# Value products in pairs, row maxima by DMA and a reordered start in an attention block (one core)

## The reference

```
q = rmsnorm(x @ q_a_w.T) @ q_b_w.T          # 16 heads of 128 + 64 (rope)
kv_a = x @ kv_a_w.T                          # 64 latent + 16 x 64 rope keys
k_nope, v = split(rmsnorm(kv_a[:64]) @ kv_b_w.T)
main = softmax(q k^T / sqrt(192)) v          # 16 heads, rope on the 64-wide parts
pattern = softmax(pq pk^T / 4) pv            # 16 heads of 16, from sp_q, sp_k, sp_v
y = gate0 * (main @ o_w.T) + gate1 * (pattern @ sp_o_w.T)
x = x + layernorm(y)
out = x + layernorm(FFN(layernorm(x)))       # 256 -> 1024 -> 256, gelu, weights quantised to MXFP4
```

## Time and profile before

| | us |
|---|---|
| median of 3 runs | 852.96 (850.64 to 856.71) |
| the profiled execution | 857.39 |
| its span | 855.6 |
| TensorE busy | 793.0 (93%) |
| VectorE busy | 587.0 (69%) |
| ScalarE busy | 403.5 (47%) |
| GpSimd busy | 429.9 (50%) |

### The profile page before, as it was taken

The page is one execution under the profiler, slowest core; times in us unless marked ns, Lnnn a source line. Parts: engine busy times, 40 slices in busy tenths (PEclk is TensorE's granted clock), DMA queues, the critical chain, the costliest instruction groups (busy, mean ns, idle before and its releaser), DMA issues. The chain is left out here.

```text
span 855.6 us, 12767 instructions
## 1 busy us (share of the span) xinstructions
PE 793.0 (93%) x4928; PEld 456.4 (53%) x4928; DVE 587.0 (69%) x669; ACT 403.5 (47%) x510; POOL 429.9 (50%) x259
## 2 busy tenths in 40 slices
PE   4878899999999999999999999999999999979984
PEld 4654555545545554555555545555555555437863
DVE  3754765666577667757775767577866689994856
ACT  3432344445555555554555455545554455531351
POOL 1414208652865475548555844584486445640233
PEclk9978899999999999999999999999999999999988
DMA  8578363005300530072017201610432413313001
GB/s 214 214 196 277 93 135 71 13 13 130 58 25 14 113 76 12 14 161 63 1 40 160 62 2 54 133 50 12 72 74 79 126 51 98 95 45 81 1 2 49
DMA packets 89024, 68.00 MB, mean 79 GB/s; under 512 B 58178, under 2 KB 67972, under 8 KB 88708
## 3 DMA queue, kind: packets, MB, share of 16 engines
q1 hardware_dynamic: 88964, 67.19, 31.0%
HBM read 41.23 MB, written 17.04 MB: 68 GB/s over the span
## 5 line engine op out<-in xcount | busy, mean ns | idle before, releaser
L991 POOL TENSOR_TENSOR acc<-acc,em 128x1024 f32<-128x1024 f32 x96 | 235.6, 2454 | 96.4 <-ACT em L1049 96.4
L1142 DVE TENSOR_REDUCE m2p<-xb 128x2 f32<-128x1024 f32 x128 | 155.2, 1220 | 79.2 <-PE xb L1300 78.9
L1150 DVE TENSOR_REDUCE m<-xb 128x2 f32<-128x1024 f32 x128 | 155.6, 1219 | 62.5 <-PE xb L1300 62.4
L1040 ACT ACTIVATE ep<-xb 128x1024 f32<-128x1024 f32 x128 | 131.1, 1024 | 112.7 <-PE xb L1300 112.7
L1049 ACT ACTIVATE em<-xb 128x1024 f32<-128x1024 f32 x128 | 131.1, 1024 | 100.7 <-PE xb L1300 91.2
L1335 PE MATMUL pvm<-em,cpair 128*64 128x512 f32 x512 | 138.2, 618 | 0.0
L954 POOL TENSOR_TENSOR rot<-rot,sin 128x512 f32<-128x512 f32 x32 | 40.9, 1279 | 116.7 <-DMA rot<-raw 116.7
L1300 PEld LDWEIGHTS xb<-pq,pk 49*128 49x128 f32 x256 | 23.8, 183 | 100.2 <-issue 81.2
L1346 PE MATMUL pvp<-ep,vp 128*32 128x512 f32 x512 | 68.2, 605 | 0.0
L991 POOL TENSOR_TENSOR acc<-em 128x1024 f32<-128x1024 f32 x16 | 38.9, 2431 | 55.5 <-PE xb L1443 50.9
L1300 PE MATMUL xb<-pq,pk 49*128 49x512 f32 x256 | 64.0, 497 | 0.0
(11 more groups left out here) (279 smaller groups left out, 1284.3 us busy)
## 6 DMA issues: line engine op xcount, KB each, us to landing
rot<-raw SPq DMA_DIRECT2D x128, 64.0 KB, 2.1
pk<-spqk_d SPq DMA_DIRECT2D x48, 128.0 KB, 4.3
sums<-rec_d SPq DMA_DIRECT2D x32, 128.0 KB, 2.9
ctx_d<-ctxr SPq DMA_DIRECT2D x14, 256.0 KB, 2.0
pq<-spqk_d SPq DMA_DIRECT2D x48, 64.0 KB, 2.3
wraw<-wst_d SPq DMA_DIRECT2D x7, 384.0 KB, 6.0
em<-in_o_w SPq DMA_DIRECT2D x1, 2048.0 KB, 7.6
vp<-vp_d SPq DMA_DIRECT2D x8, 256.0 KB, 4.5
```

What stands on the lines that cost most here:

```text
L991: pool.tensor_tensor(acc[:, :, :], before, em[:, j:j + 2, :], ALU.add).then_inc(added, 1)
L1040: act.activation(ep[:, j:j + 2, :], src[:, :, :], ACT.Exp, scale=PAT_SCALE).then_inc(ep_ready, 1)
L1142: dve.tensor_reduce(m2p[:, t, 2 * tp:2 * tp + 2, kt], src[:, :, :], AX, ALU.max).then_inc(x_dve, 1)
L1150: dve.tensor_reduce(m2[:, q, t, :, kt], src[:, :, :], AX, ALU.max).then_inc(x_dve, 1)
```

## The change

1. Row maxima no longer go through TensorE and ScalarE. The tiles mT and pT are gone. Query tiles in pm and mm take every fourth query (`t::4`), so that partition p of `ms` and `msp` holds the maxima of queries 4p to 4p + 3, and a DMA per head (`main_rows`, `pattern_rows`) writes 128 pieces of 16 bytes to one row of `mr` or `pq`. M(0) and M(8) wait for these DMAs (`mr_in`).
2. V of two half steps and PV come together at the end of even half steps.
3. The tiles of a half step are in another order: at odd ones T, pm, M, the further pm, P; at even ones pm, M, two mm, P, T. pm stand mostly at odd ones; two mm come at each even one, with `MM_LATE` 8 in place of 9.
4. The quantising is spread otherwise (`QPLAN`): 39 steps in slots 1 to 7 in place of 31, 32 in slot 8 in place of 39. Its transfers are moved to other places of SyncE's list.
5. The prologue's jobs are in another order (x is transposed first), and `xh`, `xl` are made in two halves; the gates' softmax comes earlier. In slot 0 `sk` and `sv` are made in halves, and in another order.

```diff
@@ prologue: jobs
-    jobs = [("w1T", k) for k in range(NK)] + [("spT", 0), ("spT", 1)]
-    jobs += [("kpT", k, 0) for k in range(NK)] + [("xT", k, 0) for k in range(NK)]
-    jobs += [("kpT", k, 1) for k in range(NK)] + [("xT", k, 1) for k in range(NK)]
-    jobs += [("proj1", t) for t in range(NT)]
-    jobs += [("spqk", 1, 0), ("spqk", 1, 1), ("spqk", 0, 0), ("spT", 2)]
-    for q in range(2):
-        jobs += [("pe0T", q), ("pe1T", q), ("lat0", q), ("lat1", q)]
-    for q in range(2):
-        jobs += [("cT", q), ("qm0T", q), ("qm1T", q)]
+    jobs = [("w1T", k) for k in range(NK)] + [("xT", k, 0) for k in range(NK)] + [("spT", 0)]
+    jobs += [("xT", k, 1) for k in range(NK)] + [("spT", 1)]
+    jobs += [("proj1", t) for t in range(4)] + [("kpT", 0, 0), ("kpT", 0, 1)] + [("proj1", t) for t in range(4, NT)]
+    jobs += [("kpT", 1, 0), ("spqk", 1, 0), ("spqk", 1, 1), ("kpT", 1, 1), ("spqk", 0, 0), ("spT", 2)]
+    jobs += [("pe0T", 0), ("pe1T", 0), ("lat0", 0), ("lat1", 0), ("cT", 0), ("qm0T", 0), ("qm1T", 0)]
+    jobs += [("pe0T", 1), ("pe1T", 1), ("lat0", 1), ("lat1", 1), ("cT", 1), ("qm0T", 1), ("qm1T", 1)]
...
@@ the order of tiles
-PM_STEP = [0, 0, 1, 1, 2, 1, 2, 2, 2, 2, 1, 1, 1, 0, 0, 0]
-MM_LATE = 9
+PM_STEP = [0, 0, 0, 2, 1, 3, 0, 3, 0, 3, 0, 3, 1, 0, 0, 0]
+MM_LATE = 8
...
-    if v == NP:
-        return 0 if (v, s) == (NP, 0) else 2 if (v, s) < (NP, 7) else 3
-    return 0 if v == 0 or s == 0 and v in (1, 4) else {0: 1, 13: 1, 14: 1, 15: 1 if v in (3, 7) else 2}.get(s, 0)
+    return 2 if v == NP else QPLAN.get(v, {}).get(s, 0)
...
+        if s % 2:
+            step = T + pms[0:1] + M + pms[1:] + unit
+        else:
+            mm = []
+            if s < 8:
+                if v <= NP:
+                    mm = [("mm", i) for i in (MM_LATE + s, MM_LATE + s + 1)]
+            elif v < NP:
+                mm = [("mm", i) for i in (s - MM_LATE, s - MM_LATE + 1)]
+            step = pms[0:1] + M + mm + unit + T
...
@@ rows by DMA
+            def main_rows(pair, q):
+                if pair == 0 and q == 0:
+                    sp.wait_ge(zeroed, 1)
+                sp.wait_ge(mm_ready, 2 * pair + q + 1)
+                for h in range(2):
+                    sp.dma_start(mr[64 * h:64 * h + 1, half_of(q)].rearrange("o (p t) -> o p t", t=4).bitcast(F32),
+                                 ms[:, q, h, :].bitcast(F32)).then_inc(mr_in[q], 16)
...
@@ TensorE
-                    mm = paired(out, [(pq[:, b, tp, t * P:(t + 1) * P], pk[:, b, tp, half_of(kt)])], 3 * PD)
+                    mm = paired(out, [(pq[:, b, tp, t::4], pk[:, b, tp, half_of(kt)])], 3 * PD)
...
                     if s == 0 and v >= 2:
+                        main_values(v - 2, NS - 2)
                         main_values(v - 2, NS - 1)
-                    if s and 1 <= v <= NP:
+                        pattern_values(v - 2, NT - 1)
+                    if s and s % 2 == 0 and 1 <= v <= NP:
+                        main_values(v - 1, s - 2)
                         main_values(v - 1, s - 1)
-                    if s == 1 and v >= 2:
-                        pattern_values(v - 2, NT - 1)
-                    if s >= 3 and s % 2 and 1 <= v <= NP:
-                        pattern_values(v - 1, (s - 3) // 2)
-                    if ("pT", 0) in xs[v][s] and v:
-                        x_tile(v, ("pT", 0))
+                        pattern_values(v - 1, s // 2 - 1)
```

More of the change, by code:

```diff
@@ L413, in _ @@
                 if job == ("spqk", 0, 0):
-                    for q in range(2):
-                        normalise(q)
+                    normalise(0)
+                if job == ("lat0", 0):
+                    normalise(1)
+                    dve.wait_ge(gexp, 1)
+                    link(dve.tensor_reduce(gsum[:, :], gl[:, :, :], AX, ALU.add))
+                    link(dve.reciprocal(gsum[:, :], gsum[:, :]))
+                    link(dve.tensor_tensor(gates[:, :, :], gl[:, :, :], gsum[:, :].unsqueeze(2).broadcast_to((P, NT, 2)),
+                                           ALU.mult))
                 if job == ("lat1", 0):
@@ L483, in x_steps @@
     for s in range(16):
[L484 to L503 removed]
+        T, M = ([(k, s)] if v <= NP else [] for k in "TM")
+        pms = [("pm", pm + i) for i in range(PM_STEP[s])] if v < NP else []
+        pm += PM_STEP[s]
+        unit = [("P", unit_at(v, s))] if unit_at(v, s) is not None else []
+        if s % 2:
[8 more added lines that the diff above has]
+            step = pms[0:1] + M + mm + unit + T
         if v == NP + 1 and 2 <= s < 6:
@@ L509, in x_steps @@
             step.append(("S", 0))
-        if v < NP and s == 13:
-            step.append(("pT", 0))
         steps.append(step)
@@ L586, in attention @@
         sk_hi = sem("sk_hi")
-        sk_stored = [sem(f"sk_stored{i}") for i in range(3)]
+        sk_stored = [sem(f"sk_stored{i}") for i in range(5)]
         vstored = sem("vstored")
@@ L612, in attention @@
         mrow_in = sem("mrow_in")
+        mr_in = [sem(f"mr_in{i}") for i in range(2)]
         wraw_in = sem("wraw_in")
@@ L744, in first_slot, with pattern_rows @@
                 load_minus_one(1)
+            def pattern_rows(v):
+                sp.wait_ge(pm_ready, v + 1)
+                for hh in range(4):
+                    at = 64 * (hh % 2) + 3 * PD
+                    sp.dma_start(pq[at:at + 1, v % 2, hh // 2, :].rearrange("o (p t) -> o p t", t=4).bitcast(F32),
+                                 msp[:, hh, :].bitcast(F32)).then_inc(mrow_in, 16)
+            def main_rows(pair, q):
[5 more added lines that the diff above has]
+                                 ms[:, q, h, :].bitcast(F32)).then_inc(mr_in[q], 16)
             def turn(v, u):
@@ L867, in _ @@
                         load_weights(v + 1)
-                for c in range(2):
-                    if v == 1:
-                        load_natural(0)
-                        break
-                    if v == 2 + 4 * c:
-                        store_sign(c)
-                    if v == 4 + 4 * c:
-                        load_sign(c)
+                if v == 1:
+                    load_natural(0)
                 if 1 <= v < NP:
@@ L922, in _ @@
                 if v < NP:
-                    x_emptied(sp, v, ("pT", 0))
-                    for hh in range(4):
-                        at = 64 * (hh % 2) + 3 * PD
-                        sp.dma_start(pq[at:at + 1, v % 2, hh // 2, :].bitcast(F32),
-                                     mrp[hh:hh + 1, :].bitcast(F32)).then_inc(mrow_in, 16)
+                    pattern_rows(v)
+                    main_rows(v, 0)
                 if 1 <= v < NP:
@@ L1393, in x_tile @@
                 elif kind == "sk":
-                    w, m, halves = SK[i]
-                    for j, h in enumerate(halves):
-                        mm = passes(out[:, j, :], [(spT[w][:, k, m * P:(m + 1) * P], xT[:, k, half_of(h)])
-                                                   for k in range(NK)])
+                    w, m, h = SK[i]
+                    mm = passes(out[:, 0, :], [(spT[w][:, k, m * P:(m + 1) * P], xT[:, k, half_of(h)])
+                                               for k in range(NK)])
                 elif kind == "sv":
-                    for j in range(4):
-                        t = 4 * i + j
-                        mm = passes(out[:, j // 2, j % 2 * HID:(j % 2 + 1) * HID],
+                    for j in range(2):
+                        t = 2 * i + j
+                        mm = passes(out[:, 0, j * HID:(j + 1) * HID],
                                     [(xT[:, k, t * P:(t + 1) * P], spT[2][:, k, :]) for k in range(NK)])
@@ L1428, in x_tile @@
                                            oT[:, hd, :], start=True, stop=True)
-                elif kind == "mT":
-                    pe.wait_ge(mm_ready, 2 * (v - i) + i + 1)
-                    for t in range(4):
-                        mm = pe.transpose(out[0:65, 0, t * P:(t + 1) * P], ms[:, i, t, :], ident[:, :])
-                elif kind == "pT":
-                    pe.wait_ge(pm_ready, v + 1)
-                    for t in range(4):
-                        mm = pe.transpose(out[0:4, 0, t * P:(t + 1) * P], msp[:, t, :], ident[:, :])
                 elif kind == "S":
```

126 lines of the change are left out of this document (51 added, 75 removed), and 28 rows, old and new, of the table FIRST.

## The result

| | before | changed |
|---|---|---|
| median of 20 runs | 854.33 us (849.94 to 857.73) | 858.77 us (856.04 to 863.37) |
| ratio | | 1.0054, interval 1.0039 to 1.0069 |
| the profiled execution | 857.39 | 858.00 |
| its span | 855.6 | 856.2 |
| TensorE busy | 793.0 | 782.1 |

The changed kernel is slower by 0.5%. The forecast was 858 us. (Ratios leave out two executions far above the others of their kernel: 2481 us, one of the four of the run with the old order, whose other three have the median 836.2, and 898.8, one of 17 of the kernel before beside the halved exps.) TensorE has 11 us less work and the kernel has not become shorter: that difference has to be found as waits.

What follows compares the result with a forecast made beforehand. TensorE's own queue was taken to set each slot's length. Terms -4.9 - 1.0 + 10.5 + 4 + 1.4 - 4.9 = +5.1 us on 857.39 gave 862.5; the same ratio on 852.96 gave 858 us, range 845 to 876.

Steps and rivals of the forecast that it cites:

- The mechanism: In each slot, TensorE waits for banks still being emptied; some 6.9 us of waits and restarts; chance 0.52.
- the size of the slot: Eight pairs of half steps sum to 83.9 us against 82.4: 1.5 lost per slot, 10.5 in seven.
- the front: Before the repeating slots: P(0) starts 4.9 us earlier, and M of slot 1 gains a further 1.0.
- the end: After S(15): the first output tile starts right after S, no longer waiting for the division; -4.9 us.
- the row DMAs: Row maxima sent by SyncE: hidden except in five slots, behind big transfers; +4 us, 3 of it in slot 4.
- M behind two pm: Sign in the new profile: M waits some 0.4 us by records for ScalarE's em, four times a slot.
- T behind mm, mm: Sign in the new profile: T waits for em too, five times a slot; worked out as 0.4 us.
- the 6.8 of a rope transfer: In SyncE's queue: a rope transfer behind big transfers took 6.8 us to land in place of 2.1.
- Hidden, with 1.0 us to spare: At M of half steps 0 and 8: the row lands 1.0 us before M would start anyway.
- The last slot: Slot 8: VectorE late, T and M of half step 7 wait 1.7, M of 8 another 3, rest gains 3.3; +1.4 us.
- Pairing's own worth: In each slot: eight value blocks' changes of tiling save 1.6 us and eight V at 0.05 save 0.4.
- The forecast of 862.5: Whole profiled execution: terms sum to +5.1 us against 857.39, giving 862.5, +0.6%.

Runs made afterwards that it cites:

- the run with the old order: Changed kernel with tiles and values of a half step put back as in the kernel before, one V per half step; 836.99 us, ratio 0.981.
- the halved exps: Exps on score tiles, from the fifth on, over half their columns, in both kernels: changed kernel 836.34 us (0.980), kernel before 847.13 us (0.992).
- single V: Changed kernel with one V at each half step and PV at even ones, new order of tiles kept; 860.36 us, ratio 1.009.
- pairing alone: Kernel before with only V, V, PV put together at the end of even half steps; 888.13 us, ratio 1.042.
- end only: Kernel before with four quantising steps fewer in the last slot, two instead of three at half steps 12 to 15; 851.9 us, ratio 0.998.

## Why the prediction was right

The mechanism and the size of the slot were right. That the sum came within 1 us is in part luck: the front gave less and the end more than forecast, and the row DMAs cost less, as shown below.

| term | forecast | profiled executions |
|---|---|---|
| front, to S(9) of slot 1 | -5.9 | -5.9 |
| six slots, S(9) to S(9) | +9.0, and most of the +4 | +10.6 |
| S(9) of slot 7 to the last S | +1.5 for the seventh slot, +1.4 for the last | +2.6 |
| last S to the epilogue | -4.9 | -6.9 |
| epilogue | 0 | +0.2 |
| sum | +5.1 | +0.6 |

**The slot, right to 0.2 us.** The forecast was 83.9; four of six are 83.6 to 83.9. The pairs were forecast at 10.9, 10.9, 12.3, 9.9, 10.7, 10.2, 8.2 and 10.8; in slot 4 they take 10.98, 10.85, 12.29, 9.93, 10.85, 10.24, 8.13 and 10.60. M behind two pm waits 0.65 by records, T behind mm, mm 0.18 (for the first, 0.4 by records was forecast). Put together from the runs: the rows by DMA take the slot from 82.39 to 80.45 (old order, single V), and the new order and the pairs take it to 84.16. The mechanism is shown by the halved exps. The runs with single V and with pairing alone missed their times, but by how many waits they had, and not by their kind.

**Row DMAs, mis-sized.** The term was +4, for rows behind 512 KB transfers. The landing of the row DMAs in the changed kernel:

```profile
L759 SPq DMA_DIRECT2D mr<-ms x32: 468/602/1876, 108.5 to 732.6; - x32
...
DMA to landing us min/median/max: 1.9/2.0/3.4
```

The longest is 3.4, not 6.8. M(8) waits 0.77 to 0.98 in slots 2, 3 and 4 in place of the 0.65 that the bank takes anyway: 0.6 us in all, none of it 3. The step took the 6.8 of a rope transfer for the cost of standing behind a big one, and slot 4 (83.92) is not longer than slot 2 (83.92). What the term was meant for came from elsewhere: the quantising in half step 1, 2.6 us in slots 3 and 6, which the prediction had not placed. In slot 4 the 512 KB load is issued at 403.74 and lands 4.6 later, a store of a context behind it at 409.0; the rows are issued at 405.8 and 406.3 and land at 409.2 and 409.4. So they did wait for what was ahead of them, but over 2 us of those transfers had passed when the rows were issued. The rule of the Trainium skill (DMA: Bandwidth & Descriptors, Queues, rings and completion order) agrees with this; what was mis-sized is how much of it falls on the row.

**One row not hidden.** "Hidden, with 1.0 us to spare" holds for M(0) of slots 2 to 8. In slot 0 no T, V and M stand between the last maxima and M(0), and it waits 3.12 for its row where it waited 0.56 for ScalarE. Behind this wait the granted clock is 0.52, and M(0) takes 1.3 more than before.

**The front, right in the sum only.** P(0) starts 6.45 earlier (forecast 4.9), M(0) of slot 1 6.18; it comes 63.6 behind P(0), where 61.5 was forecast. But the profiled execution of before was late here: in four other kernels with the old front P(0) starts at 52.37 to 53.56 and not at 54.23, M(0) at 115.17 to 116.61 and not at 117.52, and in the two whose slots are as before or near it (half exps, end only) S(9) comes at 168.45 and 168.51 and not at 172.18; its clock from 135 to 172 us was 0.95, theirs 1.00. Against these two the front gives 4.9 at M(0) and 2.2 at S(9), some 3 us less than forecast. With the 2.2 in place of the 5.9 the right column adds up to +4.3, the medians' +4.4. Of the 2.7 lost within slot 1, 1.3 is M(0) at clock 0.52; the forecast had 0.8 for the second mm and T(0), which now stand behind M(0). The kernel with the old order has the slow M(0) as well (3.1, at clock 0.50), behind a wait of 1.98. No run took that wait away.

**The end, more than forecast.** -4.9 was for the wait; 5.77 to 1.01 is 4.76 of it. Of the rest 0.7 is a shorter wait ahead of the epilogue (0.95 in place of 1.66) and 1.4 is the clock. Behind its idle time TensorE ran the first output tile of the kernel before at half clock, 1.2 GHz, and took 5.84 for it in place of 4.42. The stretch in the kernel before (clock 0.50):

```profile
765.70:768.50 2.80, 2.71 (x7) 2.21 (x8) 2.73 (x3) 1.49 (x3) 0.00 (x0) 0.50 0.06 10
```

and in the changed kernel (1.00, 2.4 GHz):

```profile
768.30:772.80 4.50, 4.50 (x23) 3.93 (x22) 2.67 (x3) 1.09 (x2) 0.00 (x0) 1.00 0.03 2
```

**The last slot, right in the sum only.** From T of half step 1 of slot 8 to the last S it takes 62.3 us in place of 61.2, +1.1 for a forecast of +1.4. But T and M of half step 7 wait 0.63 together and not 1.7, and M of 8 waits 0.97 for its row and not 3:

```profile
734.71 0.51 PE L1301 MATMUL xb<-qxh,kxh 64*128 64x512 f32 x2 [0.97 <-DMA mr<-ms]
```

So the rest gained 0.5 and not 3.3; in it T behind mm, mm waits 0.18 by records three times, and what else is missing was not looked into.

**Pairing's own worth** is 0.36 per pair of half steps where nothing waits, by estimate 2.9 per slot (forecast 2.0). The Trainium skill (TensorEngine Tiling (Array Packing), Key Properties) says that a change of the tiling mode drains the engine; the 0.36 for one block of values less agrees with it.

Together: the slot was right; the +4 came to 0.6 by its own cause and 2.6 by another; the end gave 2 more than forecast and the front some 3 less. The forecast of 862.5 for the profiled execution missed by 4.5, mostly because that of before was 3 us above the median of 20. In the forecast of 858 the misses nearly cancel, and that is luck.
